# Attention in whole units: a new order of scores, values and maxima on TensorE, with key loads behind the shift rows and a bias in two parts

## The chip, the cores and the metric

The kernel runs on one core of one Trainium2 chip (trn2). TensorE (PE), VectorE (DVE), ScalarE (ACT), GpSimd (POOL) and SyncE (SP) each run their own list of instructions in order and wait for each other on semaphores. The metric is the device time in microseconds of one execution of the whole program; the median of three is quoted.

## The reference, cut to what matters

A block of layers on x of 2048 tokens by 256 features: half a feed-forward layer, attention, half a feed-forward layer, twice over, with different weights and rules in the second round. The change touches the two attention layers.

```
x = x + 0.5 * L0_ffn(layernorm(x))
x = x + L0_attn(layernorm(x))      # qkv without bias, ALiBi added to the scores
x = x + 0.5 * L0_ffn(layernorm(x))
x = x + 0.5 * L1_ffn(layernorm(x))
x = x + L1_attn(layernorm(x))      # q, k, v and output with bias, rotary q and k
x = x + 0.5 * L1_ffn(layernorm(x))

# both attentions: 16 heads of 16 features, causal over 2048 tokens
scores = q @ k.T / sqrt(16) (+ bias by position);  scores[j > i] = -inf
y = softmax(scores) @ v            # per head, float32
out = y @ Wo (+ bo)
```

## The kernel before, in words

Each attention layer is one phase with its own instruction lists. "Layer one" below is the first attention (its work lies between about 190 and 725 us of the profile), "layer two" the second (about 1060 to 1620 us). A phase has three stages.

**Projections** (`projections`, L643 to L905). For each of four blocks of 512 tokens PE makes queries and keys (L709) and values (L722); in layer two a product of a row of ones with the bias row adds the bias of the values (L725), in float32. ACT and DVE split queries and keys into a high and a low part, and SP stores them to a scratch tensor in HBM (L868) in six slots: ACT may fill a slot again (L747) only when its last store has landed. SP then loads keys (`load_k`, L845) and queries (`load_q`, L1280, L1282) back in another layout. One queue, SP's, issues all of these loads and stores, in the order written.

**The main loop.** Queries are taken in blocks of 512 (`qb`, four) and heads in groups of four (`hg`, four): 16 *steps*. A step walks over key tiles of 128 keys, first the four on the diagonal, narrowed to the columns that are not masked (512, 384, 256 and 128 wide) and with the mask added by four small products (L1078), then all the full ones before it. One key tile of one step is a *unit*: 4, 8, 12 or 16 units in a step, 160 in a layer. For a unit PE makes the transposed scores of four heads as two pairs, each pair side by side in the two halves of the array (L1080); ACT takes the exponential of each head (L1246); PE multiplies these with the values of the four heads side by side (L1097) into PSUM bank 7. The scores of a head go to one of three banks, so score number i waits until exponential i-3 is done.

A softmax needs a shift. The *maxima* of a step are found ahead of it: PE makes scores the other way round for two heads and up to 512 keys (L1052, with mask products L1049 on the diagonal), and DVE takes the maximum (L1154). They use two pairs of PSUM banks in turn (`slot_bank`, the *ring*). When a step's maxima are complete, POOL cuts them in three parts (L1216 to L1222), PE transposes these (L1107, "shift rows"), ACT copies them (L1235) and SP stores them into rows of the query tile (L1290); the first scores of the step wait for that. At the end of a step ACT copies bank 7 out (L1253, "copy-out"), PE transposes it (L1116, "output") and DVE normalises it (L1181, L1184). Shift rows and outputs take their PSUM bank from the same ring as the maxima.

PE's order is written in *places*, two to a unit (L1127 to L1139): the maxima that are due, shift rows or an output where one is due, one pair of scores, then one *half of the columns* of the values of a unit 1.5 units back. Most of the time one maximum is due in a place, two a unit; while the last step of a query block works, the next block's first step has more, up to four a unit in the first block and three in some units of the second and third.

**The output projection** (`project_phase`, L1320): transposes of y, products with Wo (L1358), in layer two again a float32 product that adds the bias (L1361), and the addition to x. In layer two ACT and POOL (L1383, L1390) meanwhile split the weights of the following feed-forward layer.

## Time and profile before

| | |
|---|---|
| median of 3 executions | 1857.08 us (1843.06 to 1873.33) |
| the profiled execution | 1836.36 us |
| its span, first to last instruction | 1834.1 us |
| mean granted TensorE clock | 0.931 of full |
| busy: PE, DVE, ACT, POOL | 86%, 70%, 52%, 17% |
| groups of the two main loops, busy: maxima L1154 (DVE) / exponentials L1246 (ACT) | 665.2 / 604.3 us |
| values L1097 / maxima products L1052 / scores L1080 (PE) | 358.2 / 306.9 / 303.2 us |

The profile is of one execution. A row of the timeline gives the start and the length of an instruction, or of several alike in a row (x4 after it); the length of such a row goes from the first start to the last end. Matmuls are pipelined: the next one starts before the last has ended, so what a group of them costs is read from one start to the next, not from its length. "[0.31 <-DVE ...]" says how long the engine had stood idle and what ended that.

### The profile page before, as it was taken

Reading aid. Unit: us, or ns where it says so; the run is one execution under the profiler, and the core shown is the slowest. Engines: PE = TensorE matmul, PEld = TensorE weight load, DVE = VectorE, ACT = ScalarE, POOL = GpSimd, SP = SyncE. Lnnn points to the kernel's source line nnn. Section 1 sums busy time; section 2 is a strip of 40 time slices with the busy share of each in tenths; the row PEclk is TensorE's granted clock in tenths of the full one; section 3 lists DMA queues with packets and bytes.
Section 4 is the critical chain, followed back from the end, with each engine's and each line's share of the span. In section 5 each row is a group of like instructions: output and inputs, shape, how many; then the busy total and the mean of one; then the engine's idle time right before and its main releaser. Section 6 shows DMA issues by size and latency. Waiting matters only on the chain. (4 is left out here: it accounts for less than half of the span.)

```text
span 1834.1 us, 33102 instructions
## 1 busy us (share of the span) xinstructions
PE 1576.9 (86%) x13356; PEld 988.9 (54%) x13356; DVE 1281.7 (70%) x1859; ACT 947.4 (52%) x1889; POOL 306.4 (17%) x327
## 2 busy tenths in 40 slices
PE   1599768989989999799589789889999999997996
PEld 0487644444434444688478667444444444466885
DVE  8655646787898861555589876577788888325996
ACT  3344323667767886344334322347577678842432
POOL 5333000000000000133034423000000000030433
PEclk9999857999999999899799889679899999998998
DMA  5000877000000000100100039730000000010000
GB/s 197 24 1 1 153 172 101 28 24 13 23 13 13 2 2 1 47 1 1 58 1 0 1 102 207 93 52 21 20 11 12 21 2 2 2 70 1 12 12 24
DMA packets 37636, 70.55 MB, mean 38 GB/s; under 512 B 5190, under 2 KB 12998, under 8 KB 36423
## 3 DMA queue, kind: packets, MB, share of 16 engines
q1 hardware_dynamic: 37494, 68.58, 16.5%
q8 instruction: 100, 1.64, 0.4%
q14 instruction: 42, 0.34, 0.1%
HBM read 48.90 MB, written 22.15 MB: 39 GB/s over the span
## 5 line engine op out<-in xcount | busy, mean ns | idle before, releaser
L1154 DVE TENSOR_REDUCE l_att_maxima<-psum 128x2 f32<-128x1024 f32 (+3 forms) x640 | 665.2, 1064 | 172.8 <-PE psum L1052 165.3
L1246 ACT ACTIVATE l_att_probs<-psum 128x512 f32<-128x512 f32 (+3 forms) x1280 | 604.3, 531 | 288.1 <-PE psum L1080 268.0
L1097 PE MATMUL psum<-l_att_probs,l_att_v 128*17 128x256 f32 (+2 forms) x4608 | 358.2, 384 | 10.2 <-ACT l_att_o L1253 6.2
L1052 PE MATMUL psum<-l_kt,l_att_qt 59*128 59x512 f32 (+7 forms) x1280 | 306.9, 478 | 11.3 <-DMA l_att_qt<-qx_alibi 4.5
L1080 PE MATMUL psum<-l_att_qt,l_kt 51*128 51x512 f32 (+6 forms) x1280 | 303.2, 424 | 4.1 <-ACT l_att_probs L1246 2.6
L1052 PEld LDWEIGHTS psum<-l_kt,l_att_qt 59*128 59x128 f32 (+1 forms) x1280 | 131.5, 201 | 159.2 <-issue 89.7
L1080 PEld LDWEIGHTS psum<-l_att_qt,l_kt 59*128 59x128 f32 (+1 forms) x1280 | 155.6, 194 | 49.0 <-ACT l_att_probs L1246 32.7
L1097 PEld LDWEIGHTS psum<-l_att_probs,l_att_v 128*17 128x17 f32 x4608 | 78.4, 96 | 147.6 <-issue 83.7
L1216 POOL CAST l_att_crow<-l_att_cneg 128x16 bf16<-128x16 f32 x32 | 8.1, 252 | 855.3 <-DVE l_att_cneg L1164 855.3
L1049 PE MATMUL psum<-tri 64*128 64x128 bf16 x1024 | 81.5, 240 | 30.8 <-DVE l_att_maxima L1154 25.7
L1049 PEld LDWEIGHTS psum<-tri 64*128 64x128 bf16 x1024 | 32.2, 100 | 128.6 <-DVE l_att_maxima L1154 65.3
L1078 PE MATMUL psum<-tri 64*128 64x128 bf16 x1024 | 80.9, 230 | 0.1
L1181 DVE RECIPROCAL l_att_rinv<-psum 128x16 f32<-128x16 f32 x32 | 8.0, 250 | 96.1 <-PE psum L1116 96.1
L581 POOL TENSOR_TENSOR ffn1b_hl<-ffn1b_abs,ffn1b_hh 128x512 fp32r<-128x512 f32 x32 | 51.7, 1645 | 84.6 <-ACT ffn1b_hh L439 84.6
L581 POOL TENSOR_TENSOR ffn1a_hl<-ffn1a_abs,ffn1a_hh 128x512 fp32r<-128x512 f32 x32 | 51.7, 1643 | 84.6 <-ACT ffn1a_hh L439 84.6
L136 POOL TENSOR_TENSOR rstd<-var,mhalf 128x4 f32<-128x4 f32 x24 | 24.3, 1011 | 231.7 <-DVE var L115 231.7
L362 PE MATMUL psum<-ffn0b_xh,w_ternary 128*128 128x512 f32 x128 | 53.4, 417 | 9.2 <-DVE ffn0b_h L486 7.8
L362 PE MATMUL psum<-ffn0a_xh,w_ternary 128*128 128x512 f32 x128 | 53.2, 416 | 9.2 <-DVE ffn0a_h L486 7.8
L362 PE MATMUL psum<-ffn1b_xh,wgu_h 128*128 128x512 f32 x128 | 51.5, 403 | 3.9 <-DVE ffn1b_xl L158 2.8
L362 PE MATMUL psum<-ffn1a_xh,wgu_h 128*128 128x512 f32 x128 | 51.2, 400 | 3.9 <-DVE ffn1a_xl L158 2.8
L1078 PEld LDWEIGHTS psum<-tri 64*128 64x128 bf16 x1024 | 33.0, 98 | 38.4 <-issue 13.7
L373 PE MATMUL psum<-wdn_h,ffn1b_hh 128*128 128x256 f32 x128 | 38.8, 303 | 15.8 <-DVE x_resident L533 8.9
(201 smaller groups left out, 2922.9 us busy)
## 6 DMA issues: line engine op xcount, KB each, us to landing
l_kt<-qk_scratch SPq DMA_DIRECT2D x48, 256.0 KB, 11.6
qk_scratch<-l_att_kv_parts SPq DMA_DIRECT2D x22, 512.0 KB, 9.6
l_att_qt<-qk_scratch SPq DMA_DIRECT2D x156, 64.0 KB
qk_scratch<-y SPq DMA_DIRECT2D x10, 512.0 KB, 12.6
l_att_qt<-qk_scratch SPq DMA_DIRECT2D x12, 192.0 KB
set_raw<-in_w_gu SPq DMA_DIRECT2D x2, 1024.0 KB, 6.3
x_resident<-in_x SPq DMA_DIRECT2D x1, 2048.0 KB, 15.4
y<-in_w_gu SPq DMA_DIRECT2D x1, 2048.0 KB, 8.1
```

Source lines behind the costliest of these rows:

```text
L136: e.tensor_tensor(g.rstd[:, :], g.var[:, :], g.mhalf[:, :], ALU.pow).then_inc(s.rstd, 1)
L362: ins = e.matmul(g.ps[:, slots[c] + half, :], w_up[w][:, k, col:col + P], xp[x][:, k, :], start=k == 0 and q == 0, stop=k == KD - 1 and q ...
L373: ins = e.matmul(g.ps[:, 6 + j // 2, (j % 2) * D:(j % 2 + 1) * D], hp[x][:, u, i, j * P:(j + 1) * P], w_dn[w][:, u * GCH + i, :], start=u ...
L581: e.tensor_tensor(hl[:, c // GCH, c % GCH, :], hs[:, c // GCH, c % GCH, :], hh[:, c // GCH, c % GCH, :].bitcast(F32), ALU.subtract).then_i ...
L1049: e.matmul(g.ps[:, bank + x, w - P:w], g.tri[half, (2 + m) * P:(3 + m) * P], g.tri[half, m * P:(m + 1) * P], start=m == 0, stop=False, ski ...
L1052: e.matmul(g.ps[:, bank + x, 0:w], qt[rows_of(x), pair, t * P:(t + 1) * P], g.kt[rows_of(x), pair, c * BLK:c * BLK + w], start=c < qb, sto ...
L1078: e.matmul(g.ps[:, i % SB, off:off + P], g.tri[rows, c * P:(c + 1) * P], g.tri[rows, (2 + c) * P:(3 + c) * P], start=c == 0, stop=False, s ...
L1080: e.matmul(g.ps[:, i % SB, off:BLK], g.kt[rows_of(x), hp, kt * P:(kt + 1) * P], qt[rows_of(x), hp, off:BLK], start=u >= TPB, stop=True, sk ...
L1097: ins = e.matmul(g.ps[h * VW:h * VW + HD + 1, OB, lo:hi], g.v[:, kt, STEPS[st][1] * HG + h, :], pr[:, un % PB, h, lo:hi], start=u == 0 and ...
L1154: e.tensor_reduce(mp[:, st % 2, 2 * p:2 * p + 2, t, c], g.ps[:, bank:bank + 2, 0:w], AX.X, ALU.max).then_inc(s.mx, 1)
L1216: e.tensor_copy(cr[:, 0], whole).then_inc(s.cp, 1)
L1246: e.activation(pr[:, un % PB, h, off:BLK], g.ps[:, i % SB, off:BLK], ACT.Exp, scale=HD ** -0.5).then_inc(s.ex, 1)
```

## The change

In the main loop the place gives way to the whole unit. PE now goes: first pair of scores of unit n, values of unit n-2 in one piece of up to 512 columns, second pair of scores of unit n, all maxima due in the unit, then shift rows or an output. Layer one, PE, a stretch of steady units in the fourth query block, before (L1080 scores, L1097 values, L1052 maxima; counts are of heads):

```order
L1080 MATMUL psum<-l_att_qt,l_kt 128x512 x2
L1097 MATMUL psum<-l_att_probs,l_att_v 17x256 x4
L1052 MATMUL psum<-l_kt,l_att_qt 128x512 x2
L1080 MATMUL psum<-l_att_qt,l_kt 128x512 x2
L1097 MATMUL psum<-l_att_probs,l_att_v 17x256 x4
L1052 MATMUL psum<-l_kt,l_att_qt 128x512 x2
```

and of the change (L1087 scores, L1099 values, L1059 maxima):

```order
L1087 MATMUL psum<-l_att_qt,l_kt 128x512 x2
L1099 MATMUL psum<-l_att_probs,l_att_v 17x512 x4
L1087 MATMUL psum<-l_att_qt,l_kt 128x512 x2
L1059 MATMUL psum<-l_kt,l_att_qt 128x512 x4
L1087 MATMUL psum<-l_att_qt,l_kt 128x512 x2
L1099 MATMUL psum<-l_att_probs,l_att_v 17x512 x4
```

The values of a unit stand once and whole, and the unit's two maxima stand one behind the other at its end. The same engine where an output falls due, the third unit of a step in that block, before:

```order
L1097 MATMUL psum<-l_att_probs,l_att_v 17x256 x4
L1052 MATMUL psum<-l_kt,l_att_qt 128x512 x2
L1116 MATMUL psum<-consts,l_att_o 128x128 x4
L1078 MATMUL psum<-tri 128x128 x2
L1080 MATMUL psum<-l_att_qt,l_kt 128x256
```

and of the change (L1116 is the output in both, L1085 the mask of the scores):

```order
L1099 MATMUL psum<-l_att_probs,l_att_v 17x512 x4
L1085 MATMUL psum<-tri 128x128 x2
L1087 MATMUL psum<-l_att_qt,l_kt 128x256
L1085 MATMUL psum<-tri 128x128 x2
L1087 MATMUL psum<-l_att_qt,l_kt 128x256
L1059 MATMUL psum<-l_kt,l_att_qt 128x512 x4
L1116 MATMUL psum<-consts,l_att_o 128x128 x4
```

The output now stands behind two maxima where it stood behind one; shift rows move in the same way. On SP, layer one, from the end of the projections on, before (L868 stores, L1290 shift rows, L845 keys, L1280 and L1282 queries):

```order
L868 DMA qk_scratch<-y 128x2x512 x2
L1290 DMA l_att_qt<-l_att_ct 3x2x512 x2
L845 DMA l_kt<-qk_scratch 16x8x512 x6
L1290 DMA l_att_qt<-l_att_ct 3x2x512 x2
L845 DMA l_kt<-qk_scratch 16x8x512 x6
L1280 DMA l_att_qt<-qk_scratch 16x2x512 x6
L1282 DMA l_att_qt<-qx_alibi 11x2x512 x2
```

and of the change (L879, L1293, L854, L1283 and L1285 for the same):

```order
L879 DMA qk_scratch<-y 128x2x512 x2
L1283 DMA l_att_qt<-qk_scratch 16x4x512 x6
L1285 DMA l_att_qt<-qx_alibi 11x4x512 x2
L1293 DMA l_att_qt<-l_att_ct 3x2x512 x4
L854 DMA l_kt<-qk_scratch 16x8x512 x6
L1283 DMA l_att_qt<-qk_scratch 16x2x512 x6
L1285 DMA l_att_qt<-qx_alibi 11x2x512 x2
```

The second shift rows go ahead of the first key load, each later key load moves one step back, and the queries of the last two head groups of the first block (`4x512`), which were loaded together with those of the second group during the projections, are loaded at their end.

In layer two the bias products become two-part float32r products over 33 rows of which two hold the high and the low part of the bias; DVE prepares them with five more instructions ahead of the projections, and PE and SP's second table load wait for these (semaphore `brow`).

```diff
@@ projections, tensor
-        if small:
-            e.wait_ge(s.sm, 16 * len(small))
+        if rope:
+            e.wait_ge(s.brow, 4)
@@ projections, vector, behind dve_stats(e, g, s, 1)
+            one = g.one_col[0:HALF // 2 + 1, :]
+            e.tensor_copy(g.one_row[:, :], one.broadcast_to([HALF // 2 + 1, P]))
+            e.tensor_scalar(g.brow[:, :], one.broadcast_to([HALF // 2 + 1, 2 * D]), 0.0, None, ALU.mult).then_inc(s.brow, 1)
             e.wait_ge(s.sm, 16 * len(small))
+            e.wait_ge(s.brow, 1)
+            e.tensor_copy(g.brow[0:1, :], brow_raw[0:1, :]).then_inc(s.brow, 1)
+            e.tensor_copy(g.brow[low, :], brow_raw[low, :]).then_inc(s.brow, 1)
+            e.wait_ge(s.brow, 3)
+            e.tensor_tensor(g.brow[low, :], brow_raw[low, :], g.brow[low, :].bitcast(F32), ALU.subtract).then_inc(s.brow, 1)
@@ attention_phase
-        LAG, LEAD = 3, 4
-        PLACES = 2 * UNITS + LAG
+        LAG, LEAD = 2, 4
-        def row_place(st):
-            return maxima_place(st) + 2
-        def out_place(st):
-            return 2 * first[st + 1] + LAG + 1
+        def row_unit(st):
+            return maxima_place(st) // 2 + 1
+        def out_unit(st):
+            return first[st + 1] + LAG
@@ tensor
                 for h in range(HG):
-                    ins = e.matmul(g.ps[h * VW:h * VW + HD + 1, OB, lo:hi], g.v[:, kt, STEPS[st][1] * HG + h, :],
-                                   pr[:, un % PB, h, lo:hi], start=u == 0 and half == 0, stop=u == tiles - 1,
-                                   skip_group_check=True)
+                    ins = e.matmul(g.ps[h * VW:h * VW + HD + 1, OB, off:BLK], g.v[:, kt, STEPS[st][1] * HG + h, :],
+                                   pr[:, un % PB, h, off:BLK], start=u == 0, stop=u == tiles - 1, skip_group_check=True)
...
-            for p in range(PLACES):
-                for k in range(due(p), due(p + 1)):
+            for un in range(UNITS + LAG):
+                if un < UNITS:
+                    scores(un, 0)
+                if un >= LAG:
+                    values(un - LAG)
+                if un < UNITS:
+                    scores(un, 1)
+                for k in range(due(2 * un), due(2 * un + 2)):
                     max_products(k)
                 for st in range(1, NS):
-                    if p == row_place(st):
+                    if un == row_unit(st):
                         maxima_rows(st)
                 for st in range(NS - 1):
-                    if p == out_place(st):
+                    if un == out_unit(st):
                         output(st)
-                if p < 2 * UNITS:
-                    scores(p // 2, p % 2)
-                if p >= LAG:
-                    values((p - LAG) // 2, (p - LAG) % 2)
@@ sync
-            kv.load_k(e, 1)
             for st in range(NS):
                 qb, hg = STEPS[st]
                 if st < NS - 1:
                     rows(st + 1)
-                if st < NB - 2:
-                    kv.load_k(e, st + 2)
+                if st < NB - 1:
+                    kv.load_k(e, st + 1)
```

ACT follows: both pairs of exponentials of a unit, then a copy of shift rows where one is due; the copy-out of a step stands behind the exponentials of the second unit of the next step, where it stood between that unit's two pairs. DVE's maxima and normalisations keep their order.

## Rows read from the trace of the kernel before

**Rows 1.** Windows: length, busy of PE, PEld, DVE, ACT, POOL; clock; DMA share, GB/s

```profile
390.00:395.00 5.00, 4.77 (x38) 2.12 (x38) 3.10 (x4) 3.58 (x7) 0.00 (x0) 0.66 0.02 5
...
600.00:650.00 50.00, 49.23 (x546) 21.51 (x544) 43.10 (x42) 39.28 (x80) 1.01 (x4) 1.00 0.01 2
```

**Rows 2.** Timeline (start, length, what, [idle before]), layer one, steady, with maxima

```profile
639.51 0.50 PE L1052 MATMUL psum<-l_kt,l_att_qt 59*128 59x512 f32 x2
639.85 0.39 PE L1080 MATMUL psum<-l_att_qt,l_kt 59*128 59x512 f32 x2
640.08 3.09 DVE L1154 TENSOR_REDUCE l_att_maxima<-psum 128x2 f32<-128x1024 f32 x3 [0.19 <-PE psum L1052]
640.17 0.63 PE L1097 MATMUL psum<-l_att_probs,l_att_v 128*17 128x256 f32 x8
640.28 3.47 ACT L1246 ACTIVATE l_att_probs<-psum 128x512 f32<-128x512 f32 x6 [0.33 <-PE psum L1080]
640.73 0.50 PE L1052 MATMUL psum<-l_kt,l_att_qt 59*128 59x512 f32 x2
```

**Rows 3.** Timeline of PE: values over 128 columns

```profile
280.81 0.41 PE L1097 MATMUL psum<-l_att_probs,l_att_v 128*17 128x128 f32 x8
```

**Rows 4.** Timeline of ACT: layer one after its last maxima

```profile
678.16 6.46 ACT L1246 ACTIVATE l_att_probs<-psum 128x512 f32<-128x512 f32 x12
```

**Rows 5.** Groups of DVE by form, 450 to 650

```profile
L1154 DVE TENSOR_REDUCE l_att_maxima<-psum 128x2 f32<-128x1024 f32 x124 | 148.9, 1224 | 24.4 <-PE psum L1052 23.5
```

**Rows 6.** Timeline of PE: shift rows and outputs behind two maxima, then behind one

```profile
389.29 0.38 PE L1107 MATMUL psum<-identb,l_att_crow 128*12 128x128 bf16 x4 [1.12 <-DVE l_att_maxima L1154]
...
407.88 0.63 PE L1116 MATMUL psum<-consts,l_att_o 128*128 128x128 f32 x4 [1.05 <-DVE l_att_maxima L1154]
...
565.65 0.63 PE L1097 MATMUL psum<-l_att_probs,l_att_v 128*17 128x256 f32 x8 [0.18 <-ACT l_att_o L1253]
566.63 0.66 PE L1116 MATMUL psum<-consts,l_att_o 128*128 128x128 f32 x4
...
594.27 0.38 PE L1107 MATMUL psum<-identb,l_att_crow 128*12 128x128 bf16 x4 [0.29 <-DVE l_att_maxima L1154]
```

**Rows 7.** Timeline of ACT: one copy-out a step, both layers

```profile
377.34 0.60 ACT L1253 ACTIVATE l_att_o<-psum 128x512 f32<-128x512 f32 x1
...
404.63 0.60 ACT L1253 ACTIVATE l_att_o<-psum 128x512 f32<-128x512 f32 x1
...
1273.84 0.60 ACT L1253 ACTIVATE l_att_o<-psum 128x512 f32<-128x512 f32 x1
...
1304.24 0.60 ACT L1253 ACTIVATE l_att_o<-psum 128x512 f32<-128x512 f32 x1
```

**Rows 8.** Timeline, layer one: projection's last copy, SP's query load, PE's longest wait

```profile
243.68 0.60 ACT L747 ACTIVATE y<-psum 128x512 fp32r<-128x512 f32 x1 [5.96 <-DMA qk_scratch<-y]
...
278.35 2.64 SPq L1280 DMA_DIRECT2D l_att_qt<-qk_scratch  x6
...
295.02 0.80 PE L1052 MATMUL psum<-l_kt,l_att_qt 59*128 59x512 f32 x2 [4.50 <-DMA l_att_qt<-qx_alibi]
```

**Rows 9.** Timeline, layer two's projections: their start, one values tile with bias

```profile
1068.00 0.76 PE L709 MATMUL psum<-l_att_kv_xh,l_att_kv_w_h 128*128 128x512 f32 x1 [2.19 <-DVE l_att_kv_xl L158]
1070.28 0.17 DVE L115 TENSOR_SCALAR var<-mv 128x4 f32<-128x4 f32 x1
...
1120.15 0.39 PE L722 MATMUL psum<-l_att_kv_w_h,l_att_kv_xh 128*128 128x256 f32 x1
1121.06 0.69 PE L725 MATMUL psum<-brow,one_row 1*128 1x256 f32 x2
1121.68 0.39 PE L722 MATMUL psum<-l_att_kv_w_h,l_att_kv_xh 128*128 128x256 f32 x1
```

**Rows 10.** Timeline, layer two's output projection: POOL's chain and PE's last product

```profile
1635.93 9.38 POOL L1390 TENSOR_TENSOR wgu_l<-raw_up,wgu_h 128x1024 fp32r<-128x1024 f32 x4 [61.59 <-ACT wgu_h L1383]
...
1653.92 0.69 PE L1361 MATMUL psum<-brow,one_row 1*128 1x256 f32 x2
```

More of the change, by code:

```diff
@@ L664, in projections @@
     own = sb("parts", [P, NS if rope else NS - 4, 2, BLK], F32R)
+    low = slice(HALF // 2, HALF // 2 + 1)
     if rope:
+        brow_raw = spare[0:HALF // 2 + 1, 6, :]
+        small = small + [(brow_raw[0:1, :], a["b_row"]), (brow_raw[low, :], a["b_row"])]
         z, zb, cs = spare[:, 0:2, :], spare[:, 2:4, :], spare[:, 4:8, :].rearrange("p (b t) n -> p b t n", b=2)
@@ L863, in sync @@
                     e.wait_ge(s.za, 2 * NM * b)
+                else:
+                    e.wait_ge(s.brow, 4)
                 tables(b + 1)
@@ L1082, in scores, with values @@
                              skip_group_check=u < TPB).then_inc(s.st, 1)
-            def values(un, half):
+            def values(un):
                 st, u = where(un)
@@ L1194, in _ @@
                 maxima(k)
[L1195 to L1196 removed]
+            for un in range(UNITS + LAG):
+                for k in range(due(2 * un), due(2 * un + 2)):
                     maxima(k)
                 for st in range(1, NS):
[L1199 removed]
+                    if un == row_unit(st):
                         ring += 1
                 for st in range(NS - 1):
[L1202 removed]
+                    if un == out_unit(st):
                         normalise(st)
@@ L1256, in _ @@
             ring = due(0) - mbase[1] + 1
-            for p in range(PLACES):
-                if p < 2 * UNITS:
-                    exps(p // 2, p % 2)
-                ring += due(p + 1) - due(p)
+            for un in range(UNITS + LAG):
+                if un < UNITS:
+                    exps(un, 0)
+                    exps(un, 1)
+                ring += due(2 * un + 2) - due(2 * un)
                 for st in range(1, NS):
-                    if p == row_place(st):
+                    if un == row_unit(st):
                         rows(st, slot_bank(ring))
```

56 lines of the change are left out of this document (23 added, 33 removed).

## The prediction

> **What bounds the kernel now.** I read the windows first, then the timeline of one steady stretch, then the rows around shift rows and outputs, then the start and end of each phase. In layer one's steady main loop PE is busy 49.2 of 50 us and DVE 43.1, ACT 39.3, all at a granted clock of 1.00 [rows 1]: PE sets the pace, with DVE close behind. The timeline shows a place: maxima product, scores, values, next maxima product at 639.51, 639.85, 640.17 and 640.73 [rows 2], so 0.34 + 0.32 + 0.56 = 1.22 us, and 2.44 a unit. When the last maxima are done, twelve exponentials, three units, take 6.46 us [rows 4], 2.15 a unit, though PE's work for a unit there is only 1.76: what binds is the loop over three score banks. A score waits for the exponential three before it, so one place lasts at least 1.07: 0.43 from issue of the scores to the start of the exponential (640.28 less 639.85 [rows 2]) and by difference 0.64 for the exponential and its signal.
>
> **Values in one piece.** Values over 128 columns last 0.41 us [rows 3], over 256 columns 0.63 [rows 2], so 128 columns cost 0.215; one piece of 512 then takes 0.56 + 0.43 = 0.99 from start to start instead of 2 x 0.56 = 1.12. Per unit PE's own work becomes scores 0.32, values 0.99, scores 0.34, two maxima 0.68, together 2.33 against 2.44. Of 160 units in a layer 128 have two pieces (two diagonal and all full units of each step), so at most 0.11 x 256 = 28 us in both layers would be gained if nothing else bound.
>
> Two loops do bind. The exponential of the second pair's first head must end before the next unit's first pair is complete: 0.43 + 0.64, then scores to values 0.32, values 0.99: 2.38 a unit, maxima or not. After the last maxima, 14 full units a layer go from 2.15 to 2.38: 28 x 0.23 = **+6**. And the maxima stand in pairs. The reduction starts 0.57 us after its product (640.08 less 639.51 [rows 2]) and lasts 1.22 [rows 5], so the second of a pair ends at most 0.57 + 1.22 + 1.22 = 3.0 us after the first product, and the next unit's second maximum, wanted at 2.7, waits for that bank. With every second pair having a narrow diagonal maximum this gives a unit between 2.38 and 2.53; I take 2.48, since full pairs alternate with narrow ones. Some 84 full units in both layers then cost 84 x 0.04 = **+3** instead of gaining. In the diagonal units and the two behind them neither loop binds (exponentials are shorter): four times 0.11 on each of 32 steps and 0.3 on 24 steps, **-21**.
>
> **Shift rows, outputs, copy-outs.** Both take a bank of the ring. Behind a single maximum the wait is 0.29 for shift rows and none for the output; where the order happens to have two maxima directly ahead it is 1.12 and 1.05 [rows 6]. That is also what the sum gives: 0.57 + 1.22 less the 0.68 of two products. Now they always stand behind two. Of 15 shift rows and 14 outputs a layer some four of each already pay this: 22 x 0.65 = **+14** and 22 x 1.0 = **+22**. All of it is PE's time, because scores, values and exponentials stand queued behind the waiting instruction. The copy-out moves behind all four exponentials of the next step's second unit, and the values that wait for it come before the second pair: about 0.42 in place of 0.18 [rows 6], 30 times: **+7**. Where three maxima fall in a unit (16 units a layer) the third waits for the first's reduction inside the unit, 3.8 us; these stretches already wait today, and comparing step by step leaves **+4**. The shift rows' store is issued later relative to its step, by half a unit, but two whole units (4.8 us) remain against about 3.7 for transpose, copy, two issues and landing; no cost.
>
> **The clock.** After the waits of 386 to 390 the granted clock falls to the lower level, 1.2 GHz: 0.66 on average in the next 5 us [rows 1]. How much it costs two equal stretches show: the same eight units take 27.29 us in layer one and 30.40 in layer two, where the lower level lasted longer [rows 7]. With 1.0 and 0.4 us of waiting within one unit I expect it to fall at a few of the boundaries: **+6**, between 0 and 45.
>
> **DMA order.** In layer one ACT's last copy of the projections waits 5.96 us for a store [rows 8] that SP issued behind the query load of twelve heads. That load now carries four; 1 MB less stands ahead: **-6** (0 to -8). Layer two shows no such wait. At unit 8 PE waits 4.50 us for the queries of the second block [rows 8], issued at 278.35 behind two key loads of 1.5 MB. Now one key load is ahead, but it starts 11 us later and the queries stay behind it, and the shift rows of that step behind both; landing moves by 2 to 3 us. **-3** a layer, **-6** (+4 to -20, if the low clock that follows the wait goes as well).
>
> **Bias.** A values tile with its float32 bias takes 1.53 us, 1120.15 to 1121.68; the product starts at 1121.06, and six float32r products at 0.12 fill 0.71 of the tile [rows 9]. One float32r product of the same width is 0.12, so 0.70 a tile, 16 tiles, -11. But PE now begins only when DVE has written the bias. Today it begins at 1068.00, while DVE still has statistics to do until 1070.45 [rows 9]; behind them now stand five small instructions, no row of which exists: between 1.2 us (5 x 0.24, the tiny ones) and 3.4 (5 x 0.68, full tiles); I take 2.4, since two are one row of 512 and one a full-width write. PE starts 4.9 later and is the bound there: net **-6**. In the output projection 16 x 0.70 = 11 leave PE, whose last product starts at 1653.92; but POOL's chain of weight splits, from 1635.93 for 9.4 us and by its rate 4.7 more for the last two pieces [rows 10], starts only 2.8 (four tiles) earlier and ends at 1647.2: **-7**.
>
> **Sum:** +6 +3 -21 +14 +22 +7 +4 = +35 in the main loops, +6 clock, -6 -6 DMA, -6 -7 bias: **+16 us**. The profiled execution took 1836.36 us, its span 1834.1; the three timed ones are slower, with a median of 1857.08. The mean of all four is 1852, and I set the sum on that: **1868 us**.
>
> A rule of the Trainium skill speaks against the first term. The page "TensorE: Matmul & The Clock Gate", section "Back-to-back issue gap", gives N/2.4 + 2.5 ns from one matmul to the next, so four passes of 256 columns twice and four of 512 once would differ by 10 ns, not 130. The trace does not agree: by the widths above a group of values costs 0.13 us beyond its columns. By the page the sum would be some 26 us worse.
>
> **Rivals.**
> *The clock falls at the boundaries* (0.18, slower). For it: the fall after two waits close together [rows 1]; against it: waits of 1.0 us elsewhere at a clock that stays. The price is 3.1 a fall [rows 7]; from eight more falls on, of some 58 boundaries, the kernel is over 2% slower; a dozen give 1868 + 37 = 1905.
> *A group of values has no fixed cost* (0.07, slower). What looks like 0.13 a group is then the change of array layout and stays with the columns: 0.13 back on 256 units, less where the maxima bind, +26: 1894.
> *The waits are not PE's loss* (0.12, faster). If DVE catches up, so that shift rows and outputs find their bank free and units are bound by PE's 2.33, the terms +14, +22, +3 and the clock go, and 84 x 0.11 comes: 1868 - 45 - 9 = 1814. For it only that DVE is idle 14% of the steady loop; against it both rows with two maxima ahead.
> *The reordered loads do nothing* (0.03): the queries land as late as before, +6: 1874.
>
> **Numbers.** My forecast has 0.60; its own range is 1840 to 1895, from the bounds above. Two per cent of 1857, about what a measurement of this kernel tells from no change, is 1820 and 1894. Faster: the third rival and a little of my own lower end, 0.14. Slower: most of the clock's case, half of the second, and my upper end, 0.23. Same: 0.63. With a tenth left out on each side the range is 1822 to 1910.
>
> **What would show it.** Values of 512 columns start 0.99 us before what follows. Steady units of the fourth block last 2.4 to 2.5, those after the last maxima 2.38. Shift rows and outputs wait 1.0 to 1.1 for a maximum in every step. The wait at unit 8 is 1 to 3 us. Layer two's first projection starts near 5 us later against its phase; its output projection ends with POOL. If outputs wait less than 0.5, or units run at 2.33, the forecast is too high; if the granted clock in the fourth block is below 0.95, it is too low.

## The result, and the profile after

The changed kernel takes 1930.85 us (median of 4 runs, 1924.38 to 1938.17) against 1853.46 for the kernel before beside it: ratio 1.0438, 95% interval 1.0358 to 1.0518. It is slower, and outside the predicted range (1822 to 1910). Some executions run in a slower state of the chip and are left out of ratios and intervals, here 1873.33 us of the kernel before; the medians contain them. The profiled execution of the changed kernel took 1924.38 us, with a span of 1922.2, 88 more than before.

The first lines of the page, and its costliest groups (busy, mean ns of one, idle time before them). Line numbers have moved: scores are L1087, values L1099, maxima products L1059, reductions L1156, exponentials L1248, copy-outs L1255, shift rows L1107, outputs L1116.

```profile
span 1922.2 us, 28963 instructions
PE 1596.8 (83%) x11276; PEld 979.6 (51%) x11276; DVE 1271.2 (66%) x1864; ACT 938.6 (49%) x1889; POOL 306.9 (16%) x326
L1248 ACT ACTIVATE l_att_probs<-psum 128x512 f32<-128x512 f32 (+3 forms) x1280 | 593.5, 534 | 355.1 <-PE psum L1087 352.6
L1087 PE MATMUL psum<-l_att_qt,l_kt 51*128 51x512 f32 (+6 forms) x1280 | 380.1, 476 | 7.1 <-ACT l_att_probs L1248 6.9
L1099 PE MATMUL psum<-l_att_probs,l_att_v 128*17 128x512 f32 (+3 forms) x2560 | 332.0, 594 | 15.2 <-ACT l_att_o L1255 15.2
```

Values are busy for 332 us instead of 358, and TensorE has 2080 matmuls fewer; the scores, of which not one was added, are busy for 380 instead of 303. The mean granted clock is 0.900 where it was 0.931: (1 - 0.900) / 0.5 of the span, some 385 us, ran at 1.2 GHz, before it 253.

Where the time went is read from the copy-outs, one per step (starts of L1255; the stretches between them, in us):

| between copy-outs | 1 to 4 | 4 to 8 | 8 to 12 | 12 to 15 | 15 to 16 | all |
|---|---|---|---|---|---|---|
| before, layer one | 50.6 | 97.7 | 132.9 | 121.7 | 35.5 | 438.4 |
| after, layer one | 51.6 | 106.8 | 140.7 | 130.2 | 51.0 | 480.3 |
| before, layer two | 50.3 | 98.2 | 134.4 | 121.8 | 32.9 | 437.6 |
| after, layer two | 58.1 | 108.1 | 140.8 | 131.6 | 52.2 | 490.8 |

The main loops lose 41.9 and 53.2 us, together 95. Ahead of the first copy-out 6.6 are gained, between the layers 2.5 are lost, behind the last copy-out 2.9 are gained: 88. The largest piece is the last step, which has nothing to do but scores, exponentials and values, and which the prediction had charged with six microseconds for both layers: +34.9 (35.5 in layer one before contains 6.8 us at the lower clock, which layer two's 32.9 does not).

Windows of after: the two that answer to [rows 1], then that last step in either layer. Behind them, in a fence of its own, layer two's last step before.

```profile
390.00:395.00 5.00, 4.10 (x22) 1.50 (x24) 2.08 (x3) 1.67 (x3) 0.00 (x0) 0.50 0.01 3
600.00:650.00 50.00, 46.61 (x372) 18.92 (x373) 41.09 (x41) 36.91 (x77) 1.76 (x7) 1.00 0.01 2
715.00:756.00 41.00, 38.65 (x128) 9.32 (x131) 0.00 (x0) 21.34 (x42) 0.00 (x0) 0.50 0.00 0
1664.00:1708.00 44.00, 41.65 (x146) 10.44 (x146) 0.00 (x0) 22.77 (x44) 0.00 (x0) 0.50 0.00 0
```

```profile
1588.00:1617.00 29.00, 28.52 (x281) 11.32 (x282) 0.00 (x0) 26.62 (x55) 0.00 (x0) 1.00 0.00 1
```

In the fourth block TensorE, busy for 49.2 of 50 us before [rows 1], is now busy for 46.6: it waits. In the last step the granted clock is 0.50 for 41 and for 44 us at a stretch.

**A steady unit.** The timeline of after, where [rows 2] showed the place of 1.22 us:

```profile
642.01 1.05 PE L1099 MATMUL psum<-l_att_probs,l_att_v 128*17 128x512 f32 x8
642.99 0.50 PE L1087 MATMUL psum<-l_att_qt,l_kt 59*128 59x512 f32 x2
643.33 0.63 PE L1059 MATMUL psum<-l_kt,l_att_qt 59*128 59x512 f32 x4
643.52 2.06 ACT L1248 ACTIVATE l_att_probs<-psum 128x512 f32<-128x512 f32 x4 [0.52 <-PE psum L1087]
643.79 2.36 DVE L1156 TENSOR_REDUCE l_att_maxima<-psum 128x2 f32<-128x1024 f32 x2 [0.50 <-PE psum L1059]
643.80 0.88 PE L1087 MATMUL psum<-l_att_qt,l_kt 59*128 59x512 f32 x2
644.17 0.18 PEld L1087 LDWEIGHTS psum<-l_att_qt,l_kt 59*128 59x128 f32 x1 [0.42 <-ACT l_att_probs L1248]
644.60 1.05 PE L1099 MATMUL psum<-l_att_probs,l_att_v 128*17 128x512 f32 x8
```

Values to values is 2.59 us (644.60 less 642.01), and no engine is full. The chain through it: second pair issued 642.99, its first exponential begins 643.52 (0.53), the score that reuses its bank is issued at 644.17 (0.65 after the exponential's start), the values 0.43 behind that, the next second pair 0.98 behind them (642.99 less 642.01). 0.53 + 0.65 + 0.43 + 0.98 = 2.59. The two maxima products lie inside that chain's waits.

**The last step** is the same chain at the lower clock (TensorE's rows of after; in the third the wait has ended at 731.11):

```profile
729.63 1.22 PE L1087 MATMUL psum<-l_att_qt,l_kt 59*128 59x512 f32 x3
731.11 0.79 PE L1087 MATMUL psum<-l_att_qt,l_kt 59*128 59x512 f32 x1 [0.26 <-ACT l_att_probs L1248]
731.83 1.91 PE L1099 MATMUL psum<-l_att_probs,l_att_v 128*17 128x512 f32 x8
733.67 1.22 PE L1087 MATMUL psum<-l_att_qt,l_kt 59*128 59x512 f32 x3
```

4.04 us a unit (733.67 less 729.63), where before it was 2.15 [rows 4].

**Shift rows, outputs, copy-out** in the fourth block, rows that answer to [rows 6]:

```profile
576.99 1.05 PE L1099 MATMUL psum<-l_att_probs,l_att_v 128*17 128x512 f32 x8 [0.51 <-ACT l_att_o L1255]
580.11 0.63 PE L1116 MATMUL psum<-consts,l_att_o 128*128 128x128 f32 x4 [1.20 <-DVE l_att_maxima L1156]
...
652.93 0.38 PE L1107 MATMUL psum<-identb,l_att_crow 128*12 128x128 bf16 x4 [1.14 <-DVE l_att_maxima L1156]
```

**Unit 8 and the bias** (answers to [rows 8] and [rows 9]). The first row: the wait there is 2.40 us, for the shift rows. The others are layer two's projections: behind the statistics five small VectorE instructions from 1108.10 to 1110.33, of which the first and last stand here, and TensorE's wait for them.

```profile
286.65 0.29 PE L1085 MATMUL psum<-tri 64*128 64x128 bf16 x4 [2.40 <-DMA l_att_qt<-l_att_ct]
...
1108.10 0.21 DVE L820 CAST one_row<-one_col 33x128 fp32r<-33x128 f32 x1
...
1109.65 0.68 DVE L827 TENSOR_TENSOR brow<-y,brow 1x512 fp32r<-1x512 f32 x1
...
1110.43 0.77 PE L711 MATMUL psum<-l_att_kv_xh,l_att_kv_w_h 128*128 128x512 f32 x1 [6.88 <-DVE brow L827]
```

### The profile page after: what moved, and what is told of

The parts are those of the page before. It is cut to its first block and busy times, and to the rows that moved or that the text cites. A ratio compares the mean times of both kernels' runs of the same rounds, so it can differ in the third digit from the quotient of the medians.

```text
span 1922.2 us, 28963 instructions
## 1 busy us (share of the span) xinstructions
PE 1596.8 (83%) x11276; PEld 979.6 (51%) x11276; DVE 1271.2 (66%) x1864; ACT 938.6 (49%) x1889; POOL 306.9 (16%) x326
## 5 line engine op out<-in xcount | busy, mean ns | idle before, releaser
L1156 DVE TENSOR_REDUCE l_att_maxima<-psum 128x2 f32<-128x1024 f32 (+3 forms) x640 | 650.9, 1061 | 242.0 <-PE psum L1059 241.0
L1248 ACT ACTIVATE l_att_probs<-psum 128x512 f32<-128x512 f32 (+3 forms) x1280 | 593.5, 534 | 355.1 <-PE psum L1087 352.6
L1087 PE MATMUL psum<-l_att_qt,l_kt 51*128 51x512 f32 (+6 forms) x1280 | 380.1, 476 | 7.1 <-ACT l_att_probs L1248 6.9
L1099 PE MATMUL psum<-l_att_probs,l_att_v 128*17 128x512 f32 (+3 forms) x2560 | 332.0, 594 | 15.2 <-ACT l_att_o L1255 15.2
L1059 PE MATMUL psum<-l_kt,l_att_qt 59*128 59x512 f32 (+7 forms) x1280 | 273.6, 436 | 23.4 <-DVE l_att_maxima L1156 23.3
L1087 PEld LDWEIGHTS psum<-l_att_qt,l_kt 59*128 59x128 f32 (+1 forms) x1280 | 178.7, 203 | 218.6 <-ACT l_att_probs L1248 166.0
L1059 PEld LDWEIGHTS psum<-l_kt,l_att_qt 59*128 59x128 f32 (+1 forms) x1280 | 143.3, 206 | 45.5 <-DVE l_att_maxima L1156 42.8
L1056 PE MATMUL psum<-tri 64*128 64x128 bf16 x1024 | 88.9, 242 | 34.3 <-DVE l_att_maxima L1156 30.9
L1085 PEld LDWEIGHTS psum<-tri 64*128 64x128 bf16 x1024 | 40.1, 97 | 130.7 <-ACT l_att_probs L1248 90.5
L1085 PE MATMUL psum<-tri 64*128 64x128 bf16 x1024 | 96.4, 233 | 7.9 <-DMA l_att_qt<-l_att_ct 6.1
L1099 PEld LDWEIGHTS psum<-l_att_probs,l_att_v 128*17 128x17 f32 x2560 | 44.5, 97 | 96.2 <-ACT l_att_probs L1248 58.3
L1056 PEld LDWEIGHTS psum<-tri 64*128 64x128 bf16 x1024 | 36.6, 103 | 94.6 <-DVE l_att_maxima L1156 72.3
L580 POOL TENSOR_TENSOR ffn1b_hl<-ffn1b_abs,ffn1b_hh 128x512 fp32r<-128x512 f32 x32 | 51.6, 1643 | 84.7 <-ACT ffn1b_hh L438 84.7
L580 POOL TENSOR_TENSOR ffn1a_hl<-ffn1a_abs,ffn1a_hh 128x512 fp32r<-128x512 f32 x32 | 51.6, 1644 | 84.6 <-ACT ffn1a_hh L438 84.6
L361 PE MATMUL psum<-ffn0a_xh,w_ternary 128*128 128x512 f32 x128 | 53.2, 416 | 9.2 <-DVE ffn0a_h L485 7.8
L361 PE MATMUL psum<-ffn0b_xl,w_ternary 128*128 128x512 f32 x128 | 52.2, 408 | 0.0
```

Source lines behind the costliest of these rows:

```text
L361: ins = e.matmul(g.ps[:, slots[c] + half, :], w_up[w][:, k, col:col + P], xp[x][:, k, :], start=k == 0 and q == 0, stop=k == KD - 1 and q ...
L580: e.tensor_tensor(hl[:, c // GCH, c % GCH, :], hs[:, c // GCH, c % GCH, :], hh[:, c // GCH, c % GCH, :].bitcast(F32), ALU.subtract).then_i ...
L1056: e.matmul(g.ps[:, bank + x, w - P:w], g.tri[half, (2 + m) * P:(3 + m) * P], g.tri[half, m * P:(m + 1) * P], start=m == 0, stop=False, ski ...
L1059: e.matmul(g.ps[:, bank + x, 0:w], qt[rows_of(x), pair, t * P:(t + 1) * P], g.kt[rows_of(x), pair, c * BLK:c * BLK + w], start=c < qb, sto ...
L1085: e.matmul(g.ps[:, i % SB, off:off + P], g.tri[rows, c * P:(c + 1) * P], g.tri[rows, (2 + c) * P:(3 + c) * P], start=c == 0, stop=False, s ...
L1087: e.matmul(g.ps[:, i % SB, off:BLK], g.kt[rows_of(x), hp, kt * P:(kt + 1) * P], qt[rows_of(x), hp, off:BLK], start=u >= TPB, stop=True, sk ...
```

## Experiments

Theory A: a unit is the chain above, a score's bank held by an exponential, with the undivided values inside; what it costs is its length in the units and, through TensorE's idle time, the clock. Theory B, the prediction's own largest terms: the waits of shift rows and outputs. Each ratio is to the kernel before, measured beside it, with its 95% interval.

**1. The old order with the new bias and loads**

```diff
 # kernel after, with the loops over places and values(un, half) of before
-            for un in range(UNITS + LAG):
+            for p in range(PLACES):
```

> The kernel after, but with the old order of half units (values in two pieces of 256 columns, one maximum at a time); bias in two parts and the new order of loads stay. Theory A (all of the loss is in the new unit order; bias and loads gain what was forecast, -6 -6 -6 -7): 1828 to 1838 us, 0.985 to 0.992 of the kernel before, and the wait for the queries at unit 8 under 3 us. Theory D (the loads or the bias cost time too): 1.00 or more of the kernel before.

1841.17 us, 0.9932 (0.9885 to 0.998). The loss is in the new order, all of it: these main loops take 438.5 and 443.5 us. The gain is half of the forecast's 25. The time and TensorE's wait at unit 8, 3.10 us, are both just above what was expected.

**2. Values in two pieces, in whole-unit order**

```diff
                 if un >= LAG:
-                    values(un - LAG)
+                    values(un - LAG, 0)
                 if un < UNITS:
                     scores(un, 1)
+                if un >= LAG:
+                    values(un - LAG, 1)
```

> The kernel after, but each full unit's values in two pieces of 256 columns, one behind the first scores pair and one behind the second; maxima stay in pairs. Theory A (a unit is a loop: exponential of the second pair's first head, then the score that reuses its bank, then the values of 512 columns at 0.98 us, then the second pair: 2.59 us a unit): the loop falls to 2.2, the last step of each layer from 51 and 52 us back to 34 to 38, its low clock goes, steady units of the fourth block last 2.45 to 2.5; 1870 to 1890 us, 1.01 to 1.02 of the kernel before. Theory B (the waits of shift rows and outputs behind two maxima are the loss): these stay, and 256 more groups of values add up to 28 us: 1.045 or more.

1978.0 us, 1.0678 (1.0598 to 1.0759): slower still, against both expectations. The last step of layer one did fall, to 34.6 us, but layer two's only to 44.7, and the first fifteen steps grew. Rows of its timeline in the fourth block:

```profile
661.22 0.39 PE L1091 MATMUL psum<-l_att_qt,l_kt 59*128 59x512 f32 x2
661.54 0.63 PE L1108 MATMUL psum<-l_att_probs,l_att_v 128*17 128x256 f32 x8
661.64 2.08 ACT L1261 ACTIVATE l_att_probs<-psum 128x512 f32<-128x512 f32 x4 [0.54 <-PE psum L1091]
662.10 0.70 PE L1091 MATMUL psum<-l_att_qt,l_kt 59*128 59x512 f32 x2
662.72 0.63 PE L1108 MATMUL psum<-l_att_probs,l_att_v 128*17 128x256 f32 x8
663.28 0.50 PE L1063 MATMUL psum<-l_kt,l_att_qt 59*128 59x512 f32 x2
663.63 0.29 PE L1060 MATMUL psum<-tri 64*128 64x128 bf16 x4
663.73 0.37 PE L1063 MATMUL psum<-l_kt,l_att_qt 59*128 59x256 f32 x2
663.93 0.41 PE L1091 MATMUL psum<-l_att_qt,l_kt 59*128 59x512 f32 x2
```

A unit is 2.71 us: 0.32 + 0.56 + 0.62 + 0.56 + 0.65. The second pair takes 0.62 in place of 0.32. Some 0.10 of that comes from standing behind values and not behind a maximum (such a pair's row is 0.50 long in after, at 642.99, and 0.39 in [rows 2]); the other 0.20 is a wait: its second score needs the bank of the unit's first, whose exponential began at 661.64, and only 0.56 us of values stand between. In the old order a maximum stands there too (0.34), and that covers it [rows 2]. So the chain did not vanish with the halves; it moved to the two scores pairs, and the maxima, now all in one place, are outside it and add their full length. Layer two's first blocks also ran longer at the lower clock (mean of the whole execution 0.879), and so did its last step, for 34 us:

```profile
1726.00:1759.00 33.00, 33.00 (x202) 8.75 (x202) 0.00 (x0) 20.99 (x39) 0.00 (x0) 0.50 0.00 1
```

There TensorE is recorded as busy throughout, at 3.41 us a unit, and the clock stayed low all the same.

**3. Useless work for TensorE**

```diff
                     max_products(k)
+                if row_unit(NS - 1) < un < UNITS - TPB:
+                    fill(un)   # two pairs of 512-column products into a free bank
```

> The kernel after with work added that nothing needs: in the units of the last step of each layer that have no maxima, two pairs of products into the free bank, like two maxima products, behind the second scores pair (some 0.68 us a unit at full clock). Theory A with the clock (the last step's 51 us are a loop of 2.59 us at full clock that leaves TensorE idle, so that the granted clock falls to the lower level and the loop grows to 4.04 us): the clock stays up, units last 2.6 us, the last step falls to 36 to 40 us in each layer: 1895 to 1910 us, 1.02 to 1.03 of the kernel before. If the low clock has another cause than idle time: each unit grows or stays at 4.04 or more, and the kernel takes 1931 or longer.

1902.87 us, 1.0267 (1.0192 to 1.0342), as expected: with added work the median is 28 us below after's. The last step takes 36.7 us in both layers. Window of layer one's last step in this kernel:

```profile
711.00:745.00 34.00, 32.45 (x230) 12.63 (x229) 0.68 (x2) 26.33 (x54) 0.00 (x0) 1.00 0.00 1
```

The clock is 1.00 throughout, and the full units last 2.59 us. So of the last steps' 34.9 us, (51.0 - 36.7) + (52.2 - 36.7) = 29.8 are the clock and 5.1 the rest, the longer unit above all.

**4. Values between the two scores of the first pair**

```diff
                 if un < UNITS:
-                    scores(un, 0)
+                    scores(un, 0, (0,))
                 if un >= LAG:
                     values(un - LAG)
                 if un < UNITS:
+                    scores(un, 0, (1,))
                     scores(un, 1)
```

> The kernel after, but the values stand between the first and the second score of the first pair instead of behind both; values stay in one piece of 512 columns, maxima in pairs. Theory A (loop through the score bank): the score that waits for the exponential now comes behind the values, the loop no longer holds them, and a steady unit falls from 2.59 to 2.35 to 2.5 us; last step 34 to 40 us; 1865 to 1890 us, 1.005 to 1.02. Theory B (waits behind two maxima) or a cost of one more change between scores and values: units of 2.6 or more, and 1.04 or more of the kernel before.

1997.8 us, 1.0753 (1.066 to 1.0845): theory A, as I applied it, failed here, and the result is what was written down for theory B or for the price of one more change between scores and values. This run by itself doesn't tell these apart from a chain that was followed wrongly; the rows do. TensorE:

```profile
664.80 0.52 PE L1087 MATMUL psum<-l_att_qt,l_kt 59*128 59x512 f32 x2
...
666.01 0.49 PE L1087 MATMUL psum<-l_att_qt,l_kt 59*128 59x512 f32 x1
666.43 1.05 PE L1099 MATMUL psum<-l_att_probs,l_att_v 128*17 128x512 f32 x8
667.42 0.73 PE L1087 MATMUL psum<-l_att_qt,l_kt 59*128 59x512 f32 x3
```

664.80 to 667.42 is 2.62, the chain again: first score behind the values, exponential, score ahead of the values 1.21 later, values 0.42 behind it. Seen afterwards, it had to be so. With four scores between one group of values and the next and three banks, the last score ahead of the values always reuses the bank of the first behind the previous ones, wherever the values stand. Why the unequal steps grew by as much as they did (120.0 between copy-outs 4 and 8 of layer two, 108.1 in after) was not followed up.

**5. Five score banks in the last step**

In short (the waits for the exponentials follow the banks):

```diff
+        def score_bank(i):   # i % 3 as before, until the last maxima are read
+            k = i - 4 * U5
+            return i % SB if k < 0 else (4, 6, 4 * U5 % SB, (4 * U5 + 1) % SB, (4 * U5 + 2) % SB)[k % 5]
```

> The kernel after, but once the last maxima of a layer are read (some 14 units a layer), the scores go round five banks instead of three: two banks of the maxima's ring are free there. Unit order, values of 512 columns and everything before that point stay. Theory A (the loop score, exponential, score in the same bank, values, next pair holds a unit at 2.59 us, and the clock's fall, which makes it 4.04, only follows from TensorE's idle time): the loop opens, the units last 2.06 to 2.2 us, set by the four exponentials, at full clock; the last step falls from 51 and 52 us to 31 to 35: 1890 to 1900 us, 1.02 to 1.027 of the kernel before. If the clock falls on its own there and the banks are not the bound: units of 3.3 us or more, 1.035 or more.

1877.86 us, 1.0156 (1.0083 to 1.0228), somewhat better than expected. Both last steps take 29.4 us, which is less than before (35.5 and 32.9), at 1.91 us a unit. Their window in layer one:

```profile
709.00:736.00 27.00, 26.57 (x190) 8.82 (x182) 0.68 (x2) 25.01 (x54) 0.00 (x0) 1.00 0.00 1
```

ScalarE is busy for 25.0 of 27 us: the four exponentials now set the pace, 1.91 / 4 = 0.48 each. So the three banks were the bound of the last step, and with the bound gone the clock stayed up. The other stretches are within 3 us of after's.

**6. Shift rows and outputs ahead of the maxima**

```diff
-                for k in range(due(2 * un), due(2 * un + 2)):
-                    max_products(k)
                 for st in range(1, NS):
                     ...
                         output(st)
+                for k in range(due(2 * un), due(2 * un + 2)):
+                    max_products(k)
```

> The kernel after, but shift rows and outputs stand ahead of the unit's two maxima instead of behind them. Theory B (their waits of 1.0 to 1.2 us behind two maxima are TensorE's loss, as forecast +36): those waits go, and 20 to 35 us with them: 1895 to 1912 us, 1.024 to 1.033 of the kernel before. Theory A (the unit's loop sets the pace and the wait only moves to the maxima that now come behind): no more than 10 us less, 1.038 to 1.046.

1890.38 us, 1.0156 (1.0051 to 1.0261). The median is below even what theory B wanted (1895 to 1912), but the traces divide it. Between copy-outs 12 and 15 a layer gains 1.6 and 3.0 us, and all stretches ahead of the fifteenth together 7.9 and 10.3: more than the 10 us that theory A allowed, less than theory B's 20 to 35. The rest of layer one's gain, 14.8 us, is its last step, which nothing was done to, and which this time kept its clock (why this one did and layer two's didn't is not shown):

```profile
701.00:734.00 33.00, 28.38 (x186) 9.13 (x182) 0.68 (x2) 25.64 (x53) 0.00 (x0) 1.00 0.00 1
1629.00:1673.00 44.00, 41.44 (x143) 10.35 (x147) 0.00 (x0) 23.11 (x45) 0.00 (x0) 0.50 0.00 0
```

```profile
714.90 0.73 PE L1087 MATMUL psum<-l_att_qt,l_kt 59*128 59x512 f32 x3
716.08 0.49 PE L1087 MATMUL psum<-l_att_qt,l_kt 59*128 59x512 f32 x1 [0.45 <-ACT l_att_probs L1248]
716.50 1.05 PE L1099 MATMUL psum<-l_att_probs,l_att_v 128*17 128x512 f32 x8
717.48 0.73 PE L1087 MATMUL psum<-l_att_qt,l_kt 59*128 59x512 f32 x3
```

The same units, without a maximum, take 2.58 us at full clock (717.48 less 714.90) in layer one and 4.04 at half in layer two. This is the chain shown bare: its length is the same with two maxima in a unit and with none. So at most 18 us of the 36 forecast for both kinds of wait could be had back; in the fourth block it is 0.5 to 0.6 us a step of waits that last 1.14 and 1.20, and the rest is waited for by what now stands behind.

**7. and 8. One part alone.** Bias in two parts on the kernel before, and the new loads on the kernel before:

```diff
 # 7: only brow, one_row (33 rows, float32r) and their waits
-            e.wait_ge(s.sm, 16 * len(small))
+            e.wait_ge(s.brow, 4)
 # 8: only the sync engine's order, and its semaphores
-                    load_q(0, HG, HEADS - HG, s.qrest)
+                elif part == 1:
+                    load_q(0, HG, HG, s.qnext)
+                else:
+                    load_q(0, 2 * HG, HEADS - 2 * HG, s.qrest)
...
-            kv.load_k(e, 1)
...
+                if st < NB - 1:
+                    kv.load_k(e, st + 1)
```

> The kernel before with the bias in two float32r parts as its only change. As forecast, -6 in the projections of layer two (each values tile 0.7 us shorter, start 5 us later) and -7 in its output projection: 0.991 to 0.995 of the kernel before. If the later start or another engine takes the first gain back: the projections' end moves by less than 2 us and the ratio is 0.995 to 0.999.

> The kernel before with the new order of loads as its only change (queries of the first block in three parts, shift rows ahead of the key loads). As forecast, -6 at the start of layer one's main loop and -3 in each layer at unit 8: 0.992 to 0.996 of the kernel before, the wait for the queries of the second block from 4.5 us to 1 to 3. If the queries land as late as before: only the first 6 us, 0.996 to 0.998, and the wait at unit 8 stays.

Bias: 1848.32 us, 1.0011 (0.9972 to 1.005). Loads: 1843.01 us, 0.9953 (0.9914 to 0.9991). A values tile of the kernel with the new bias (compare [rows 9], 1.53 us):

```profile
1129.16 0.39 PE L724 MATMUL psum<-l_att_kv_w_h,l_att_kv_xh 128*128 128x256 f32 x1
...
1130.06 0.38 PE L727 MATMUL psum<-brow,one_row 33*128 33x256 f32 x1
1130.37 0.39 PE L724 MATMUL psum<-l_att_kv_w_h,l_att_kv_xh 128*128 128x256 f32 x1
```

1.21 us, so 0.32 less, not 0.70. From the first to the last product with weights the projections take 75.1 us, before 80.3; but they start 5 us later against the statistics, and the first exponential of the main loop comes 441.3 us behind the sixteenth copy-out of layer one, before 440.9: no gain. In the output projection the last product with weights comes 31.1 us behind the last copy-out, before 35.7: -4.6. With the loads alone the first copy-out of layer one is at 277.75 instead of 283.71, -6.0 as forecast, and the wait at unit 8 is 3.53 us instead of 4.50, above the 1 to 3 that were expected:

```profile
288.10 0.59 PE L1053 MATMUL psum<-l_kt,l_att_qt 59*128 59x512 f32 x2 [3.53 <-DMA l_att_qt<-qx_alibi]
```

**9. Two pieces right behind each other**

```diff
+                for lo, hi in [(off, mid), (mid, BLK)] if BLK - off > 2 * P else [(off, BLK)]:
                     for h in range(HG):
-                        ... pr[:, un % PB, h, off:BLK] ...
+                        ... pr[:, un % PB, h, lo:hi] ...
```

> The kernel after, but a full unit's values are issued as two pieces of 256 columns right behind each other, at the same place; nothing else moves. Theory A (the values stand in the loop that sets the unit) and a fixed cost of 0.13 us a group: the values' 0.98 us become 1.12 and the steady unit of the fourth block goes from 2.59 to 2.72. Rival, as in the prediction (no fixed cost: the 0.13 us belong to the change between scores and values): 0.98 and 2.59 stay. If the values were not in the loop, 2.59 stays although they last 1.12.

```profile
643.31 1.06 PE L1101 MATMUL psum<-l_att_probs,l_att_v 128*17 128x256 f32 x16
644.29 0.50 PE L1087 MATMUL psum<-l_att_qt,l_kt 59*128 59x512 f32 x2
```

Sixteen matmuls of 256 columns take 0.98 us, as eight of 512 do, and the unit stays at 2.59 to 2.60 (one run, 1930.08 us). A group has no fixed cost of its own; by exclusion the 0.13 us are the change between scores and values, which the whole-unit order saves. That settles my weighing of the rule in the Trainium skill, "TensorE: Matmul & The Clock Gate", section "Back-to-back issue gap": for matmuls of one kind right behind each other it agrees with this run. The rule does not speak of what a change between groups costs.

**10., 11. and 12. What can be kept.** The old order of run 1 with five banks in the last step; the same with TensorE's wait for the bias moved; the whole-unit kernel with the edits of runs 5 and 6 together.

```diff
 # 11: in the projections of the values
                 if rope:
+                    if is_first(b) and j == 0:
+                        e.wait_ge(s.brow, 4)
                     ins = e.matmul(dst, g.one_row[:, :], g.brow[:, 0:D], start=False, stop=True)
```

> The old order of half units with bias in two parts, the new order of loads, and five score banks once the last maxima are read. Theory A: the three banks bind the old order there too (2.17 us a unit in the last step); with five, units of 1.91 as in the whole-unit kernel with five banks, 3 to 5 us a layer: 0.986 to 0.990 of the kernel before. If something else binds: 0.993 as with three banks.

> The same, and TensorE waits for the bias only ahead of the first product that reads it, behind the first block's four pairs of projections, not ahead of all projections. If the start of 5 us later is what took the bias's gain: 3 to 5 us less than with the early wait, 0.984 to 0.988 of the kernel before. If VectorE, which has the same five instructions ahead of its first eviction, sets the start anyway: no difference to the early wait.

> The whole-unit kernel after with both repairs: shift rows and outputs ahead of the unit's maxima, and five score banks once the last maxima are read. If the two effects are separate: 1855 to 1868 us, 1.003 to 1.010 of the kernel before, steps of the fourth block at 43.2 to 43.4 us (41.3 before) and both last steps at 29 to 31. What then remains against the old order with the same bias and loads is the unit of 2.59 us in place of 2.44 and the boundaries, some 10 to 20 us in the two main loops. If the waits only hid each other: no better than the five banks alone, 1.0156.

| run | median us | ratio, 95% interval |
|---|---|---|
| 10, old order, five banks | 1833.76 | 0.9921 (0.9884 to 0.9958) |
| 11, and the later wait | 1825.06 | 0.9899 (0.9846 to 0.9953) |
| 12, whole units, both repairs | 1854.0 | 1.0013 (0.9978 to 1.0048) |

In run 10 both last steps take 30.7 us at 1.91 a unit (run 1: 34.2 and 32.9), 3.5 and 2.2 less where 3 to 5 a layer were expected; the ratio is above what was expected, and by the intervals it can't be told from run 1. In run 11 layer two's first exponential comes 436.2 us behind the sixteenth copy-out instead of 440.7: the later wait gives 4.5 back. Its ratio, too, is above what was expected (0.984 to 0.988). It has the lowest median here, ahead of both kernels that were given, by 1.0% of the kernel before; by the intervals it can't be told from run 10. Run 12 is level with the kernel before, somewhat better than expected. Its last steps take 29.4, but between copy-outs 12 and 15 it needs 126.4 and 126.5 where run 10 needs 121.0: the chain of the steady units and the boundaries, about 1.8 us a step, remain. That is not the largest part: in the profiled executions its main loops are 43 us longer than run 10's, where 10 to 20 were expected, and 36 of them lie between copy-outs 4 and 12, where some units have three maxima.

## Why the prediction was wrong

The forecast was +16 us on the profiled execution; it was +88. Three terms failed: the chain of a unit, put at 2.38 us, is 2.59; the clock of the last step, put at nothing, cost 29.8 us; and units with three maxima, put at +4, cost some 13 to 18. Point by point, the sums of units from the exponentials' starts in both layers:

**The unit's chain was mis-sized.** "0.43 + 0.64, then scores to values 0.32, values 0.99: 2.38 a unit" measured 2.59. The values are right (0.98), and so is the exponential with its signal (0.65). The two hand-overs of the scores were read from pairs that stand behind a maximum [rows 2]. In the new order the second pair stands behind values, and 0.53 us pass to its exponential for 0.43; and the score that waited for its bank stands alone before the values, 0.43 ahead of them for 0.32. So the steady full unit is 2.59, not 2.48, and above the old 2.44; units 6 to 11 of the fourth block's first three steps cost 92.0 us for 87.7, +4.3 where 36 x 0.04 = 1.4 was forecast.

**The last step: right in mechanism, wrong by the clock.** "After the last maxima ... 28 x 0.23 = +6" is near what run 3 shows at full clock (+5.1), but that the sizes agree is luck: a full unit there grew by 0.42 (2.17 to 2.59), not by 0.23, but only some nine of a layer's 14 did (9 x 0.42 = 3.8, as layer two went from 32.9 to 36.7), and layer one's last step before, 2.6 longer than layer two's, held some low clock. But in 2.59 us TensorE has 0.98 + 0.32 + 0.34 = 1.64 us of work there; the clock fell with the first full units of the last step (at 715 us in layer one, behind waits of 0.50 and 0.45 us), and stayed down for 41 and 44 us: +29.8. Why it fell there is in part argued: useless work (run 3) and two more banks (run 5) kept it up, but in run 6 the same waits in layer one didn't bring it down. I had looked for its fall only at the boundaries, "+6, between 0 and 45", at 3.1 a fall; the rival of 0.18 had the right cause in the wrong place. This term alone would have carried the forecast from 1868 to about 1890.

**The diagonal units gained unevenly.** Units 3 to 5 of a step went from 6.95 to 5.93 us in the third block (tenth step), more than was forecast for them, but only from 7.0 to 6.8 in the fourth, where the reductions are as many and wider. That the reductions are the reason wasn't tested, and how much of the -21 came was not separated.

**Shift rows, outputs, copy-outs** wait as forecast: 1.14, 1.20 and 0.51 us. In the fourth block's first three steps units 0 to 2, with the output, cost +7.6 (+1.27 a step), and the last four, with the shift rows, +6.5 (+1.08; 1.3 of the 6.5 is a fall of the clock in layer two's fourteenth step); in the tenth step +1.38 and nothing (-0.05). The forecast had +43 for 30 steps, 1.43 each: right for the third block, 0.7 to 0.9 too little for the fourth, where the last four units also contain some of the longer chain.

**Three maxima in a unit** were the other miss: "+4". Units 4 to 7 of the seventh step to 3 of the eighth, and 8 of the eleventh to 6 of the twelfth, cost 155.6 us instead of 132.5. Eight boundaries lie in them, some 5 to 10 us at the prices above; the other 13 to 18 are the third maximum, which waits 0.84 to 1.12 for VectorE inside the unit, with the scores behind it, and part of it at the lower clock. How much is each was not separated. Two rows of after, the three maxima of the eleventh step's last unit in layer one:

```profile
527.42 0.62 PE L1059 MATMUL psum<-l_kt,l_att_qt 59*128 59x512 f32 x4
529.16 0.50 PE L1059 MATMUL psum<-l_kt,l_att_qt 59*128 59x512 f32 x2 [1.12 <-DVE l_att_maxima L1156]
```

**The start.** Of the first block +7.8 us (copy-outs 1 to 4) fall on layer two, where the clock is low for 41 us on end. Run 1 has the old order there and loses 7.0 in the same place, with 44 us of low clock, and run 10, with the same order and 20 us of low clock, loses nothing (48.8): this goes with the clock and not with the order.

**Loads:** -6 in layer one right; at unit 8 -1.0 in run 8 and -1.4 in run 1, for -3. In after the shift rows are what TensorE waits for there, 2.40 us, a wait that the prediction had only in the words "and the shift rows of that step behind both".

**Bias:** the start 4.9 us later was right (5), the tile's gain was not: 0.32, since the float32r product still costs 0.31 with the change of operand shape around it, and I had priced it like its neighbours, 0.12, and taken the steps beside it, 0.21 and 0.22, for as short. 16 x 0.32 = 5.1 and the delay cancel. Output projection -4.6 for -7.

**The rivals.** "The waits are not PE's loss": true for about half of them, as run 6 shows (18 of 36 us came back), but a unit never ran at 2.33. "A group of values has no fixed cost": true (run 9), and still without its price, because the change between scores and values is what is saved. "The clock falls at the boundaries" is dealt with above; "the reordered loads do nothing" fell with run 8, though the queries land only 1.0 us earlier.

## What to carry to other kernels

Before work is merged into longer pieces, follow each buffer round its loop: who frees it, who stands behind the instruction that waits for it, and how long the undivided piece in that loop is. With n banks and more than n users between two such pieces, the loop contains the piece wherever it is put, and only further banks, or fewer users between smaller pieces, open it. An order in which TensorE waits in every unit for tens of microseconds is to be charged with the lower clock as well, at least as a risk; where the idle time can't be removed, products that nobody reads can be cheaper than none. And a wait measured on an engine is a gain only if what stands behind it doesn't wait for the same thing.

## What the runs showed of the hardware

- The same stretch of instructions ran at either level of the clock in one execution: 2.58 us a unit at 2.4 GHz in layer one and 4.04 at 1.2 GHz in layer two (run 6). At the lower level TensorE is busy for 41.4 of 44 us, so that it hardly shows the idle time by which a reader would find the cause; at the higher it is busy for 28.4 of 33. The low clock lengthens values (0.98 to 1.84) and scores, and the loop with them.
- Work that nothing needs kept the clock at 1.00 in the last steps and made a kernel 28 us faster (run 3).
- A busy TensorE does not by itself lift the clock: in run 2 it stayed at 1.2 GHz for 34 us with TensorE recorded as busy for 33.0 of 33. What lifts it these runs don't show.
- Values in 16 matmuls of 256 columns or 8 of 512: 0.98 us both (run 9). A group of values between scores costs 0.13 us beyond its columns (two groups of 256 columns 2 x 0.56 [rows 2], for 0.98).
- A float32r bias product over 256 columns between products of another shape costs 0.31 us, the float32 one 0.62 [rows 9].
- Exponentials of 128x512 that need not wait follow each other every 0.48 us (run 5), though one is recorded as 0.6 us long or longer: they overlap.
